# The rounding of a network's weights in the last unit of the attention ahead of it, and two turns of one context in one stage

## The reference

```
x = x + L0_xattn(ctx_1024, layernorm(x), ...)    # takes layer_norm(ctx_1024) * w + b
...                                              # layers 1 to 3 take ctx_1024 itself, without a norm
x = x + L3_xattn(layernorm(x), ctx_1024, ...)
x = x + L3_ffn(layernorm(x), w1, conv_w, conv_b, w2)

def weight_quant(w):                             # w1 and w2: 1024 x 256 and 256 x 1024
    scale = 1.0 / clip(mean(abs(w)), 1e-05)
    return clip(round(w * scale), -1, 1) / scale
```

## Time and profile before

| | |
|---|---|
| time, median of 3 runs | 2333.49 us (2326.95, 2333.49, 2333.94) |
| the profiled execution: its time, its span | 2336.61 us, 2334.6 us |
| mean granted TensorE clock | 0.886 |
| busy: PE, PEld, DVE, ACT, POOL | 1864.1, 936.3, 1477.6, 1073.5, 831.4 us |

### The profile page before, as it was taken

One profiled execution on the slowest core, in us unless ns is written; L12 is line 12 of the kernel. 1 busy time (PEld: TensorE's weight loads), 2 busy tenths in 40 slices (PEclk: granted clock), 3 DMA queues, 4 the chain that ended last, 5 costly groups with the idle time before them and its releaser, 6 DMA issues. The chain is left out here.

```text
span 2334.6 us, 32209 instructions
## 1 busy us (share of the span) xinstructions
PE 1864.1 (80%) x11381; PEld 936.3 (40%) x11381; DVE 1477.6 (63%) x2553; ACT 1073.5 (46%) x1818; POOL 831.4 (36%) x751
## 2 busy tenths in 40 slices
PE   6787979999876667667896687999779776999844
PEld 3344423333543444445583452333248433222223
DVE  4444256664666999995435448999554464877386
ACT  2343124444333454452344243888833433366636
POOL 1000025555144999994204012666640412000012
PEclk8888989999886998997897798999989887799967
DMA  6511462110019115002425715221044302523000
GB/s 193 151 29 41 162 225 64 62 34 14 19 63 234 15 20 87 2 1 110 153 84 171 185 42 134 60 60 39 13 185 155 128 10 55 118 59 60 10 1 18
DMA packets 172352, 190.50 MB, mean 82 GB/s; under 512 B 14820, under 2 KB 138798, under 8 KB 171286
## 3 DMA queue, kind: packets, MB, share of 16 engines
q1 hardware_dynamic: 169124, 180.07, 28.0%
q0 software_dynamic: 3072, 8.39, 1.1%
HBM read 124.04 MB, written 68.30 MB: 82 GB/s over the span
## 5 line engine op out<-in xcount | busy, mean ns | idle before, releaser
L3391 POOL TENSOR_TENSOR a2x_masked<-a2x_masked,tall_rows 128x512 f32<-128x512 f32 x128 | 163.5, 1278 | 111.7 <-ACT a2x_masked L3353 111.7
L1389 ACT ACTIVATE experts<-a1x_scores 128x1024 f32<-128x1024 f32 x128 | 124.1, 1021 | 160.9 <-PE a1x_scores L1320 160.9
L3402 DVE TENSOR_REDUCE a3x_row_most<-a3x_ring 128x1 f32<-128x512 f32 x256 | 159.4, 683 | 43.5 <-PE a3x_ring L3249 43.5
L3402 DVE TENSOR_REDUCE a2x_row_most<-a2x_ring 128x1 f32<-128x512 f32 x256 | 162.5, 680 | 7.8 <-PE a2x_ring L3252 7.7
L1426 POOL TENSOR_TENSOR a1x_tree<-experts 128x1024 f32<-128x1024 f32 x64 | 150.5, 2352 | 29.2 <-ACT experts L1389 28.6
L662 POOL TENSOR_TENSOR a0x_pair_sums<-a0x_probs_T 128x1024 f32<-128x1024 f32 x48 | 114.8, 2391 | 129.0 <-ACT a0x_probs_T L791 101.6
L845 DVE TENSOR_REDUCE ctx_then_heads<-a0x_rows 128x2 f32<-128x1024 f32 x88 | 107.7, 1224 | 81.6 <-PE a0x_rows L680 81.4
L1358 DVE TENSOR_TENSOR experts<-experts,a1x_inverse_total 128x2048 f32<-128x2048 f32 x64 | 145.7, 2277 | 4.2 <-ACT a1x_inverse_total L1402 4.2
L3346 ACT ACTIVATE a3x_probs_T<-a3x_scores_T 128x1024 f32<-128x1024 f32 x128 | 123.2, 1018 | 48.2 <-PE a3x_scores_T L3276 48.1
L1309 PE MATMUL a1x_scores<-a1x_qs,a1x_ks 96*128 96x128 bf16 x1024 | 91.7, 242 | 58.5 <-ACT experts L1389 45.1
L3346 ACT ACTIVATE wide_rows<-a2x_masked 128x1024 f32<-128x1024 f32 x128 | 135.9, 1062 | 1.4 <-POOL a2x_masked L3391 1.4
(11 more groups left out here) (676 smaller groups left out, 4272.4 us busy)
## 6 DMA issues: line engine op xcount, KB each, us to landing
v_scr<-p0x_vout SPq DMA_DIRECT2D x24, 256.0 KB, 2.0
k_scr<-p0x_x SPq DMA_DIRECT2D x24, 256.0 KB, 2.3
ctx_then_heads<-k_scr SPq DMA_DIRECT2D x8, 768.0 KB
a0x_vs<-v_scr SPq DMA_DIRECT2D x8, 768.0 KB, 4.7
experts<-in_L_ffn_w SPq DMA_DIRECT2D x8, 768.0 KB, 6.6
v_scr<-experts SPq DMA_DIRECT2D x16, 256.0 KB, 2.2
a1x_vs<-v_scr SPq DMA_DIRECT2D x16, 256.0 KB, 5.3
v_scr<-m1f_vout SPq DMA_DIRECT2D x16, 256.0 KB, 2.2
```

The lines of the kernel that those rows point to most:

```text
L1389: nc.scalar.activation(ex[:, n % E, 8 * half:8 * half + 8, :], sp_[:, g % 3, :, :, :].rearrange("p i j q -> p (i j) q"), ACT.Exp).then_inc ...
L3391: nc.gpsimd.tensor_tensor(sm[:, i % 2, 1, :], sm[:, i % 2, 1, :], full[1][:, i // 2 % KT, :], ALU.add).then_inc(pool_masked, 1)
L3402: nc.vector.tensor_reduce(rm[:, u % 2, h * QT + qt:h * QT + qt + 1, part], ring[:, row_place(r) % 3, 0:n], AX.X, ALU.max).then_inc(row_mos ...
```

## The change

Two edits that have nothing to do with each other.

First, the stage `ctxT` is gone, and `media` does its work too: PE turns the raw tiles into four PSUM banks of their own (`raw`) and ACT copies them to `core.ctxT`, both ahead of what they did in this stage before. DVE writes the normed tiles over `ctxs`, so it waits, once for every four tiles, until PE has turned them.

Second, the stages `wq1` and `wq2` are gone. Their DVE instructions, for both weights in pairs, stand in DVE's program of `a3x` between `scale(6)` and `scale(7)`; the sum over partitions is one matmul with two columns, into the ring bank that the last two `turn_u` don't use, and stands in PE's program at step N - 3 = 61, behind the second half of the scores. In the diff, a comment at the right names the engine whose program it is.

```diff
-def norm_stage(core, name, src, xn, xnT, w=None, b=None, loads=(), norm=True, far=(), tiles_in=()):
+def norm_stage(core, name, src, xn, xnT, w=None, b=None, loads=(), far=(), tiles_in=(), raw_T=None):
+        raw = st.ps("raw", [P, 4, 512]) if raw_T is not None else None
...
                 for t in range(tiles):                                                        # DVE
+                    if raw_T is not None and t % 4 == 0:
+                        dve.wait_ge(raw_turned, KH * (t // 4 + 1))
                     nc.vector.tensor_scalar(xn[:, t, :], src[:, t, :], mv[:, t, 0:1], rstd[:, t:t + 1],
                                             ALU.subtract, ALU.mult).then_inc(xn_done, 1)
...
                 nc.scalar.activation(first_root[:, :], core.ident[:, 0:1], ACT.Sqrt)          # ACT
+                for i in range(groups * KH if raw_T is not None else 0):
+                    g, k = divmod(i, KH)
+                    act.wait_ge(raw_turned, i + 1)
+                    nc.scalar.copy(raw_T[:, k, g * 512:(g + 1) * 512], raw[:, i % 4, :]).then_inc(raw_moved, 1)
                 act.wait_ge(var_ready, 1)
                 nc.scalar.activation(std[:, :], mv[:, :, 1], ACT.Sqrt).then_inc(std_ready, 1)
...
+                for i in range(groups * KH if raw_T is not None else 0):                      # PE
+                    g, k = divmod(i, KH)
+                    if i >= 4:
+                        pe.wait_ge(raw_moved, i - 3)
+                    for t in range(4):
+                        mm = nc.tensor.transpose(raw[:, i % 4, t * P:(t + 1) * P], src[:, 4 * g + t, k * P:(k + 1) * P],
+                                                 core.ident[:, :])
+                    mm.then_inc(raw_turned, 1)
...
+        sums = ring[:, ({0, 1, 2} - {u_place(U - 2) % 3, u_place(U - 1) % 3}).pop(), 0:2]
...
+                        if quant is not None and n == N - 3 and half == 1:                    # PE, a3x
+                            pe.wait_ge(weight_step, 2)
+                            pe.wait_ge(row_most, U * NR)
+                            pe.wait_ge(shift_ready, U)
+                            nc.tensor.matmul(sums, core.ones[:, :], part[:, :], start=True, stop=True
+                                             ).then_inc(weighed, 1)
...
+                if quant is not None:                                                         # DVE, a3x
+                    (w1, w2), rounded, means = quant
+                    dve.wait_ge(loaded, 16 * len(loads))
+                    for i, w in enumerate((w1, w2)):
+                        nc.vector.tensor_reduce(part[:, i:i + 1], w, AX.X, ALU.add, apply_absolute_value=True
+                                                ).then_inc(weight_step, 1)
+                    dve.wait_ge(weighed, 1)
+                    nc.vector.tensor_scalar(means, sums, 1.0 / (P * w1.shape[1]), 1e-5, ALU.mult, ALU.max
+                                            ).then_inc(mean_ready, 1)
+                    dve.wait_ge(mean_ready, 1)
+                    nc.vector.reciprocal(inv_mean[:, :], means).then_inc(mean_ready, 1)
+                    dve.wait_ge(mean_ready, 2)
+                    for i, w in enumerate((w1, w2)):
+                        nc.vector.tensor_scalar(w, w, inv_mean[:, i:i + 1], ROUND, ALU.mult, ALU.add
+                                                ).then_inc(weight_step, 1)
+                    for i, w in enumerate((w1, w2)):
+                        dve.wait_ge(weight_step, 3 + i)
+                        nc.vector.tensor_scalar(w, w, ROUND - 1, ROUND + 1, ALU.max, ALU.min).then_inc(weight_step, 1)
+                    for i, w in enumerate((w1, w2)):
+                        dve.wait_ge(weight_step, 5 + i)
+                        nc.vector.tensor_scalar(rounded[i], w, ROUND, None, ALU.subtract).then_inc(weight_step, 1)
                 scale(U - 1)
...
-            norm_stage(core, "ctxT", ctxs, None, core.ctxT, norm=False)
-            norm_stage(core, "media", ctxs, ctxs, mT, core.col("L0_xattn_ln_media_w"), core.col("L0_xattn_ln_media_b"))
+            norm_stage(core, "media", ctxs, ctxs, mT, core.col("L0_xattn_ln_media_w"), core.col("L0_xattn_ln_media_b"),
+                       raw_T=core.ctxT)
...
-        weight_quant_stage(core, "wq1", w1f, w1q[:, :, :].rearrange("p k n -> p (k n)"), means[:, 0:1], core.ones[:, :])
-        weight_quant_stage(core, "wq2", w2f, w2q[:, :, :].rearrange("p k n -> p (k n)"), means[:, 1:2], core.ones[:, :])
```

More of the change, by code:

```diff
@@ L164, in norm_stage @@
         first_root = st.sb("first_root", [P, 1])
+        raw_turned, raw_moved = st.sem("raw_turned"), st.sem("raw_moved")
         tp = st.ps("tp", [P, 4, 512])
+        raw = st.ps("raw", [P, 4, 512]) if raw_T is not None else None
         with nc.Block() as block:
@@ L175, in _ @@
                 end_prefetch(sp, loads, loaded)
[L177 to L194, removed]
+            @block.vector
+            def _(dve):
+                for t in range(tiles):
+                    if tiles_in:
+                        dve.wait_ge(tile_in[t], 16)
+                    nc.vector.bn_stats(stats[:, t, :], src[:, t, :]).then_inc(stats_done, 1)
+                dve.wait_ge(stats_done, tiles)
+                for t in range(tiles):
+                    nc.vector.bn_aggr(mv[:, t, :], stats[:, t, :]).then_inc(aggr_done, 1)
+                dve.wait_ge(aggr_done, tiles)
+                nc.vector.tensor_scalar(mv[:, :, 1], mv[:, :, 1], EPS, None, ALU.add).then_inc(var_ready, 1)
+                dve.wait_ge(std_ready, 1)
+                nc.vector.reciprocal(rstd[:, :], std[:, :]).then_inc(rstd_ready, 1)
+                dve.wait_ge(rstd_ready, 1)
+                for t in range(tiles):
+                    if raw_T is not None and t % 4 == 0:
+                        dve.wait_ge(raw_turned, KH * (t // 4 + 1))
+                    nc.vector.tensor_scalar(xn[:, t, :], src[:, t, :], mv[:, t, 0:1], rstd[:, t:t + 1],
+                                            ALU.subtract, ALU.mult).then_inc(xn_done, 1)
             @block.scalar
@@ L199, in _ @@
                     act.wait_ge(ident_in, 16)
[L200 to L206, removed]
+                nc.scalar.activation(first_root[:, :], core.ident[:, 0:1], ACT.Sqrt)
+                for i in range(groups * KH if raw_T is not None else 0):
+                    g, k = divmod(i, KH)
+                    act.wait_ge(raw_turned, i + 1)
+                    nc.scalar.copy(raw_T[:, k, g * 512:(g + 1) * 512], raw[:, i % 4, :]).then_inc(raw_moved, 1)
+                act.wait_ge(var_ready, 1)
+                nc.scalar.activation(std[:, :], mv[:, :, 1], ACT.Sqrt).then_inc(std_ready, 1)
                 for i in range(groups * KH):
@@ L230, in _ @@
                         mm = nc.tensor.transpose(tp[:, i % 4, t * P:(t + 1) * P],
-                                                 (xn if norm else src)[:, 4 * g + t, k * P:(k + 1) * P],
+                                                 xn[:, 4 * g + t, k * P:(k + 1) * P],
                                                  core.ident[:, :])
@@ L2735 @@
 ROUND = 1.5 * 2.0 ** 23
[L2738 to L2771, removed]
 def token_quant(dve, nc, step, n0, x, amax, scale, back, rounded):
@@ L3113, in quad_attention_stage @@
                          turn_most_at, nbuf=3, extra=0, q_rows=None, k_rows=None, key_mask=None,
-                         query_mask=None, full=None, probs=None, loads=()):
+                         query_mask=None, full=None, probs=None, loads=(), quant=None):
     nc = core.nc
@@ L3167, in quad_attention_stage @@
         u_moved, u_turned, inverse, ao_done = (st.sem(x) for x in ("u_moved", "u_turned", "inverse", "ao_done"))
+        weighed, mean_ready, weight_step = (st.sem(x) for x in ("weighed", "mean_ready", "weight_step"))
         qs, ks, rm, mcol, shift, first_exp = bufs
+        part = st.sb("weight_part", [P, 2]) if quant is not None else None
+        inv_mean = st.sb("inverse_mean", [P, 2]) if quant is not None else None
         vs = st.sb("vs", [P, 2, KT, P])
@@ L3785, in program @@
     stack = {"q_parts": scr["q_scr"], "k_parts": scr["k_scr"]}
-    with nc.sbuf_tensor("ao3x", [P, NT, C], F32) as ao:
+    with nc.sbuf_tensor("ao3x", [P, NT, C], F32) as ao, nc.sbuf_tensor("w1q", [P, KH, 1024], BF16) as w1q, \
+            nc.sbuf_tensor("w2q", [P, 8, C], BF16) as w2q, nc.sbuf_tensor("means", [P, 2], F32) as means:
         with quad_buffers(core, "a3x", S) as bufs:
@@ L3795, in program @@
         out_norm_stage(core, "o3x", ao, wo, core.xn, None)
-    if upto == 11:
-        return
-    with nc.sbuf_tensor("w1q", [P, KH, 1024], BF16) as w1q, nc.sbuf_tensor("w2q", [P, 8, C], BF16) as w2q, \
-            nc.sbuf_tensor("means", [P, 2], F32) as means, \
-            nc.sbuf_tensor("hT", [P, 8, B, T], F32) as hT:
-        weight_quant_stage(core, "wq1", w1f, w1q[:, :, :].rearrange("p k n -> p (k n)"), means[:, 0:1], core.ones[:, :])
```

(8 more changed lines are left out.)

7 lines of the change are left out of this document (3 added, 4 removed).

## The result

Over five runs each, the changed kernel took 2311.37 us in the median (2308.81 to 2315.32), the kernel before 2333.49 (2326.95 to 2334.11). The ratio is 0.9916 with a 95% interval of 0.9899 to 0.9934: faster by 19.6 us (15.4 to 23.6); the medians are 22.1 apart. The forecast was 2313.6, with a range of 2307 to 2320. The profiled execution took 2311.37 us with a span of 2309.5, 25.1 less than the span before. One execution of the kernel of e11 (2565 us) and two of the kernel before beside it (2457 and 3611 us) were far off all others and stand in no ratio and no median.

What follows compares the result with a forecast made beforehand. Bound by the longest engine chain between barriers: PE/ACT and DVE alternate in the context, DVE works alone in the weight stages. Gains of 7.0 + 12.9 = 19.9 us from 2333.49 make 2313.6, range 2307 to 2320.

Steps and rivals of the forecast that it cites:

- The first edit: Context: statistics start 7.26 us earlier, root 0.22 us late behind raw copies; 7.04 us gained, taken as 7.0, from 6.7 to 7.6.
- Rival (c): Context: raw turns and statistics hold each other up, only the 0.31 us barrier goes; 2320.3 us, chance 0.04.
- The reductions and the matmul: `a3x`: two reductions, 4.58 us, end 2.2 us before PE's place for the matmul, so PE doesn't wait.
- The price of the matmul on PE: `a3x`: 0.3 to 0.6 us straight onto the stage, but beside DVE's longer work.
- The passes: `a3x`: six DVE passes in pairs overlap slightly and take 7.0 us, at most 7.7.
- Rival (a): `a3x`: passes don't overlap and the matmul costs its old price; 2.9 us given back; 2314.6 us, chance 0.20.
- Given back: End of `a3x`: the reciprocal of `scale(7)` starts 1.9 us later, at least 1.5, at most 2.9.
- `o3x`: Starts later after longer PE idling; a lower clock for one or two products costs up to 0.6 us, taken as 0.2.
- Rival (b): Network, `b1` and `b2`: PE gets its full clock earlier, gaining 3.4 us; 2310.2 us, chance 0.10.
- The sum: Whole kernel: 7.0 us from the context plus 12.9 us from the weights, 19.9 us gained.
- Rival (d): `p0x`: PE's clock falls, each us of full-clock work costing another; 2343.6 us with 30 us of it, chance 0.04.

Runs made afterwards that it cites:

- e11: The kernel of e9 timed again, unchanged: ratio 0.9909 to the kernel before, median 2312.50 us of five runs.
- e6: Changed kernel with the weight instructions early as in e3, and ACT's root ahead of the last raw copy: ratio 0.9896 to the kernel before, median 2307.23 us.
- e1: Kernel before with the first edit (the context) alone: ratio 0.9977 to the kernel before, median 2326.08 us.
- e7: Changed kernel with PE's raw turns waiting until the variances are there: ratio 0.9951 to the kernel before, median 2320.82 us.
- e9: Changed kernel with PE's matmul of the partial sums one step sooner, at N - 4: one run, 2319.98 us beside 2331.07.
- e3: Changed kernel with PE's matmul at N - 9 and DVE's weight instructions right behind the last row maxima: ratio 0.9898 to the kernel before, median 2307.55 us.
- e12: Changed kernel with five more, unused matmuls of the partial sums on PE behind `turn_u(7)`: ratio 0.9918 to the kernel before, median 2314.73 us.
- e10: Changed kernel with three passes over `w1`, then three over `w2`, instead of in pairs: one run, 2316.34 us beside 2331.07.

## Why the prediction was right

**The first edit.** 7.04 us were forecast, 6.97 measured. The root's wait for the last copy was 0.20 us (0.22 forecast), and e6 took it back. The mechanism came true, but that the number is right to 0.07 us is partly luck: the clock fell just as the turns of the normed tiles began, as the sum had assumed. With the clock full there, e1 gained 8.1 us, outside the term's 6.7 to 7.6. Rival (c), two readers in each other's way, fell with the statistics' 5.32 us, the same as before, and with e7.

**The reductions and the matmul.** The sums were ready at 2190.47, PE took the matmul up only after the scores of 2192.39, so it didn't wait, as forecast. The price of the matmul on PE, 0.3 to 0.6 us "straight onto `a3x`", was wrong: it took 0.28 us in the rows and cost nothing, here and in e9. It lay in a gap of PE. The row at 2204.06 in the earlier trace rows has 1.27 us for four scores, of which two alone take 0.61, so the second two started 0.66 us behind the first; with the matmul between them they started 2193.06 - 2192.39 = 0.67 us behind. The exponentials came no later either. It changed nothing in the sum, as DVE's end was the later one.

**The passes.** 7.0 us forecast from the maxima's overlap, 6.93 measured. Rival (a) fell: an instruction starts 1.14 us after one of 1.22 if it needn't wait. Given back were 1.71 us where 1.9 were forecast, since the first pass started 1.7 us ahead of the last exponential (2193.55 and 2195.24) and not 1.6 (2205.3 and 2206.90), and the passes took 6.93 and not 7.0.

**`o3x`.** Forecast 0.2, at most 0.6, measured 0.87: this term was mis-sized. The windows of `o3x` in the kernel before, and then in the changed kernel, show the half clock:

```profile
2211.40:2213.40 2.00, 0.69 (x5) 0.51 (x6) 0.00 (x0) 1.95 (x4) 0.10 (x1) 1.00 0.00 0
2213.40:2217.00 3.60, 3.60 (x11) 2.90 (x12) 1.03 (x3) 0.74 (x3) 0.00 (x0) 0.53 0.00 0
2217.00:2227.20 10.20, 7.12 (x34) 4.92 (x32) 9.04 (x37) 3.47 (x12) 0.00 (x0) 1.00 0.00 0
```

```profile
2201.50:2202.20 0.70, 0.63 (x4) 0.40 (x4) 0.00 (x0) 0.70 (x1) 0.10 (x1) 0.93 0.00 0
2202.20:2209.00 6.80, 5.62 (x17) 4.54 (x18) 2.11 (x7) 2.34 (x7) 0.00 (x0) 0.51 0.00 0
2209.00:2218.10 9.10, 6.03 (x29) 4.21 (x27) 8.04 (x34) 3.21 (x11) 0.00 (x0) 1.00 0.00 0
```

Before, the clock was full for `o3x`'s first 2 us and half for 3.4; after, it was full for 0.6 us only and then half for 6.8. That an idle PE ahead is the cause was my theory. For it: with the matmul early (e3, e6, e11) the half clock is back at 3.4 us. Against it: e9 had 16.5 us without more idle time, by another place of the fall, and e12 didn't shorten it. What is shown is that `o3x` goes with how much of it falls into half clock: 15.8 us with 3.4 us of it, 16.4 to 16.7 with 6.8 or more, in all fourteen profiles. Whether PE's idle time or the stage's later start does it stays open.

**The network.** Rival (b) was given 3.4 us and one chance in ten; a third of it came, in every profile without the weight stages. Timeline of `b1` before, then after:

```profile
2258.47 2.02 PE L2867 MATMUL b_bp<-ident,b_back 128*128 128x128 f32 x8
2260.28 1.55 PE L2850 MATMUL b_pp<-b_qT,w1q 128*128 128x512 bf16 x4
```

```profile
2234.30 1.11 PE L2840 MATMUL b_bp<-ident,b_back 128*128 128x128 f32 x8
2235.24 1.03 PE L2823 MATMUL b_pp<-b_qT,w1q 128*128 128x512 bf16 x4
```

The eight turns of the token scales take 1.11 us instead of 2.02 and the four products 1.03 instead of 1.55. The clock was full there for 6.8 us from 2232.83 on; before, it was full for 3.4 us from 2261.34 on, when these turns were done. The first eight products ran at half clock in both, so the other part of (b) didn't come.

**The sum.** It was 19.9 us by the forecast and 20.4 by the rows. Three errors stand behind that: -0.7 in `o3x`, +1.0 in `b1`, which the sum left out, and +0.2 in what `a3x` gave back. That the first two nearly cancel is luck. The medians are 22.1 us apart; the 1.7 beyond the rows are the spread of the runs, which the interval of 15.4 to 23.6 takes in.

**Rival (d)** didn't show: the granted clock of 196 to 300 us, most of it `p0x`, was 0.98 (0.95 before, where more of the context's stages lies in these microseconds).

## What to carry to other kernels

Where stages meet at barriers, look for one that only one engine works in, and for a hole of that engine in a neighbour; the gain is the stage's length less what runs past the hole's end, and both can be read before the change. Put such work at the start of the hole, not at its end: 1.7 us were lost only because PE's matmul stood late (e9 and e11). Write independent instructions of one engine in pairs, so that none waits for the one just before it; here that was worth 0.5 us (e10).

## What the runs showed of the hardware

Two profiles of the same code can differ by 11.0 us in 2300, 9.4 of it in the first 190 us, with a granted clock of 0.83 or 0.90 there, while the stages behind `a3x` repeat to 0.1 us in these two. They needn't: e9 and e11, one kernel too, differ by 0.8 us in `o3x` and by 0.3 in `b1` and `b2`. The difference of two spans would have given the change 25.1 us; 20.4 are its own.

The fall of the granted clock behind `a3x` came 6.6 to 7.0 us after the last exponential in thirteen of the fourteen profiles, whatever the kernel did in between, though other stages had shifted by up to 11 us. In e9 it came after 5.0. So `o3x`, when it starts 1.7 us later, meets the fall nearer to its own start, and it took 0.8 to 0.9 us more; that the later start is the cause is likely by e12 but not shown.
